# A mixture-of-experts kernel whose routed experts take groups of 512 tokens in place of tiles of 128

## The reference, cut to what matters

```python
# x is (8, 512, 512), cond (8, 512), all float32; 8 blocks of 512 tokens
ae = layernorm(cond) * ln_g + ln_b
xw = gelu(ae @ cw1 + cb1) @ cw2 + cb2            # (8, 2*512*8): x_a, x_b of rank 8
layer = base + einsum('bdr,bkr->bdk', x_a, x_b)
x = x + (x + einsum('btc,bco->bto', x, layer))   # x1, (4096, 512) as tokens

shared = silu(x @ w1) * (x @ w3) @ w2            # 512 -> 1024 -> 512
s = sigmoid(concat(x, cond) @ router_W)          # (4096, 8)
top2 of s + router_bias; gates = the two s, divided by their sum
h = gelu(x @ W1e[e]); y = h @ W2e[e]             # 8 experts, 512 -> 512 -> 512
routed = sum over the two chosen experts of gate * y
x = x + (shared + routed) / 3
```

## Time and profile before

| | us |
|---|---|
| median of three runs | 1197.51 |
| lowest to highest | 1196.04 to 1203.25 |
| the profiled execution, its own time | 1202.75 |
| its span, first to last instruction | 1200.9 |
| TensorE busy | 1160.2 (97%) |
| VectorE, ScalarE, GpSimd busy | 416.4, 287.8, 188.1 |

### The profile page before, as it was taken

How to read it: one execution, slowest core, us unless ns; L and a number is a source line. 1 busy time by engine, 2 the same in 40 slices (tenths; PEclk the granted TensorE clock), 3 DMA queues, 4 the chain that set the end, 5 groups by cost and what they waited for, 6 DMA issues and landing times.

```text
span 1200.9 us, 18241 instructions
## 1 busy us (share of the span) xinstructions
PE 1160.2 (97%) x5762; PEld 935.4 (78%) x5763; DVE 416.4 (35%) x812; ACT 287.8 (24%) x498; POOL 188.1 (16%) x207
## 2 busy tenths in 40 slices
PE   6999898899999999999999998999999999999998
PEld 5666676778788888888888887888888888888887
DVE  4104653535233333333333334233333314233334
ACT  2212453521222222222222222121211112121211
POOL 2002165642510000000000003202020010202020
PEclk8999999899999999999999999999999999999999
DMA  8562589895332222222222224404031130404031
GB/s 309 227 239 95 207 299 347 289 306 162 129 118 83 79 87 79 79 87 79 82 84 83 83 79 123 175 1 175 1 100 74 39 136 0 175 0 175 0 125 49
DMA packets 70480, 151.82 MB, mean 126 GB/s; under 512 B 9753, under 2 KB 18457, under 8 KB 68658
## 3 DMA queue, kind: packets, MB, share of 16 engines
q1 hardware_dynamic: 57666, 111.55, 26.9%
q0 software_dynamic: 12784, 39.86, 9.4%
HBM read 88.73 MB, written 62.65 MB: 126 GB/s over the span
## 4 chain that ended last, share of the span: by engine, by line
PE 91%; DVE 4%; DMA 2%; POOL 1%; issue 1%; ACT 1%; SPq 0%; DVEq 0%; ACTq 0%
PE L L1375 7%; PE L L1377 7%; PE L L1376 7%; PE Rb L1377 7%; PE Rb L1375 7%; PE Rb L1376 7%; PE M L1375 5%; PE M L1376 5%; PE M L1377 5%; PE K L1376 5%; PE K L1375 5%; PE K L1377 5%; PE Rb L1465 3%; PE K L1703 2%; PE K L1660 2%; PE M L1403 2%
## 5 line engine op out<-in xcount | busy, mean ns | idle before, releaser
L752 POOL DMA_INDIRECT yb<-ys_d,pos_fix x64 | 61.2, 957 | 326.6 <-DVE xres L1324 308.6
L1375 PE MATMUL L<-weh,xgh 128*128 x260 | 107.6, 414 | 1.8 <-issue 1.8
L1276 DVE TENSOR_TENSOR xgl<-K,xgh 128x512 fp32r<-128x512 f32 x66 | 45.7, 692 | 173.4 <-ACT xgh L897 173.4
L1375 PE MATMUL Rb<-weh,hTh 128*128 x256 | 105.5, 412 | 0.0
L1375 PE MATMUL K<-x1h,w13h 128*128 128x512 f32 x256 | 101.6, 397 | 3.0 <-DVE x1l L1355 3.0
L1375 PE MATMUL M<-w2h,gTh 128*128 128x512 f32 x256 | 102.3, 399 | 2.3 <-DVE gTl L460 2.3
L1377 PE MATMUL L<-weh,xgl 128*128 x260 | 102.7, 395 | 0.0
L1376 PE MATMUL L<-wel,xgh 128*128 x260 | 102.5, 394 | 0.0
L1376 PE MATMUL K<-x1l,w13h 128*128 128x512 f32 x256 | 102.0, 398 | 0.0
L1376 PE MATMUL M<-w2l,gTh 128*128 128x512 f32 x256 | 101.9, 398 | 0.0
L1377 PE MATMUL M<-w2h,gTl 128*128 128x512 f32 x256 | 101.8, 398 | 0.0
(11 more groups left out here) (238 smaller groups left out, 2146.1 us busy)
## 6 DMA issues: line engine op xcount, KB each, us to landing
xr<-xs_d SPq DMA_DIRECT2D x68, 256.0 KB, 2.6
w2c<-in_L_cond_w_dram SPq DMA_DIRECT2D x8, 2048.0 KB, 8.5
ys_d<-yo SPq DMA_DIRECT2D x64, 256.0 KB, 2.1
xtok<-in_x_dram SPq DMA_DIRECT2D x32, 256.0 KB, 7.4
x_d<-x1tok SPq DMA_DIRECT2D x8, 1024.0 KB, 7.9
xres<-x_d SPq DMA_DIRECT2D x8, 1024.0 KB, 9.5
x1T_d<-xp SPq DMA_DIRECT2D x7, 1024.0 KB, 4.6
out_dram<-xres SPq DMA_DIRECT2D x7, 1024.0 KB, 4.8
```

The lines of the kernel that those rows point to most:

```text
L752: pool.indirect_dma_start(out=yb[:, c, :], out_offset=None, in_=ys_d, in_offset=bass.IndirectOffsetOnAxis(ap=pos_fix[:, c:c + 1].bitcast(U ...
L1276: tt(xgl[:].rearrange("p k n -> p (k n)"), TX[:], xgh[:].rearrange("p k n -> p (k n)").bitcast(F32), ALU.subtract).then_inc(xg_lo, 1)
L1375: mm(o, ah, bh_, start=start, stop=False)
```

## The change

Experts take groups of GR = 512 tokens. In place of the rows, GpSimd scatters token numbers (4 bytes) into `idx_d`; for each group it loads 512 numbers and gathers the rows from `x1_d` (4 indirect DMAs) into `xg`. SP spreads `xg` over `xr` by 16 DMAs of 32 partitions each, such that VectorE's transposes of 32 x 32 blocks finish the turning (the columns of x1 lie permuted in `x1_d` for this). The first product has W1 as the stationary operand and gives h already turned, so TensorE does no transposes. Each group loads W1 and W2 of its expert anew, in four quarters each, which ScalarE and VectorE split. The sum goes to `total`, apart from `xres`, and its first term is added in four parts of 128 columns. `pass_group(g, n)` does group g and prepares n = g + 1.

```diff
-    TILES = (N * TOPK + E * (P - 1)) // P
+    GR = TT * P
+    REGION = N + GR
+    GROUPS_MAX = (N * TOPK + E * (GR - 1)) // GR
...
+        def groups(eng, body):
+            last = value(eng, LAST, 0, GROUPS_MAX - 1, 1)
+            with eng.Fori(0, last) as g:
+                body(g, g + 1)
+            body(last, None)
...
@@ SP
-            def load_rows(t, slot):
-                row = value(sp, ROW, t, E * REGION)
-                sp.dma_start(xr[:, slot], xs_d[ds(row, P), :]).then_inc(xr_in[slot], 16)
+            def load_e1(g, m):
+                row = value(sp, EROW, g, (E - 1) * KC)
+                sp.dma_start(weraw[:, m].rearrange("p (k n) -> p k n", k=KC),
+                             w1e_view[:, ds(row, KC), m * P:(m + 1) * P]).then_inc(weraw_in[m], 16)
+            def spread_rows(g):
+                sp.wait_ge(xg_in, g * (16 * TT) + 16 * TT)
+                for j in range(4):
+                    for i in range(4):
+                        sp.dma_start(xr[32 * j:32 * j + 32, :, i], xg[32 * i:32 * i + 32, :, j * P:(j + 1) * P]
+                                     ).then_inc(xr_in, 16)
+            def load_group(g, n):
+                    sp.wait_ge(xt_f, n * TT)
+                    spread_rows(n)
+                    for m in range(KC):
+                        sp.wait_ge(e2_lo, g * KC + m + 1)
+                        load_e1(n, m)
+                    for m in range(KC):
+                        sp.wait_ge(e1_lo, n * KC + m + 1)
+                        load_e2(n, m)
...
+                store_y(g, 0)
+                store_y(g, 1)
@@ GpSimd
-                            out=xs_d, out_offset=bass.IndirectOffsetOnAxis(ap=pos_int[:, c:c + 1].bitcast(U32), axis=0),
-                            in_=x1tok[i][:, t, :], in_offset=None).then_inc(scat[i], 16)
+                            out=idx_d, out_offset=bass.IndirectOffsetOnAxis(ap=pos_int[:, c:c + 1].bitcast(U32), axis=0),
+                            in_=tokid[:, n:n + 1], in_offset=None).then_inc(ids_out, 16)
+            for t in range(N * TOPK // P, GROUPS_MAX * TT):
+                pool.dma_start(ys_d[t * P:(t + 1) * P, :].rearrange("r (k c) -> r k c", k=KC), zero_src).then_inc(ys_zero, 16)
...
+            pool.wait_ge(S.sum_ps, TT)
+            def gather_rows(g):
+                row = value(pool, ROW, g, E * REGION - GR)
+                pool.dma_start(idx[:], idx_d[ds(row, GR), :].rearrange("(t p) o -> p (t o)", p=P),
+                               allow_slow_non_contiguous=True).then_inc(idx_in, 16)
+                pool.wait_ge(idx_in, g * 16 + 16)
+                for t in range(TT):
+                    pool.indirect_dma_start(
+                        out=xg[:, t, :], out_offset=None, in_=x1_d,
+                        in_offset=bass.IndirectOffsetOnAxis(ap=idx[:, t:t + 1].bitcast(U32), axis=0)).then_inc(xg_in, 16)
+            def gather_group(g, n):
+                    pool.wait_ge(xr_in, n * 256)
+                    gather_rows(n)
@@ ScalarE
+            def pass_group(g, n):
+                cut_e2(g, 0)
+                cut_e2(g, 1)
+                gelu(g, 0)
+                cut_e2(g, 2)
+                gelu(g, 1)
+                cut_e2(g, 3)
+                    cut_e1(n, 0)
+                gelu(g, 2)
+                    cut_e1(n, 1)
+                gelu(g, 3)
+                    cut_x(n, 0)
...
@@ VectorE
+            def turn_rows(g, t):
+                dve.wait_ge(xr_in, g * 256 + 256)
...
+                nc.vector.transpose(xt[:, t % 2].rearrange("p c (i n) -> p i c n", i=4),
+                                    xr[:, t].rearrange("p i (c f) -> p i c f", c=KC)).then_inc(xt_f, 1)
@@ TensorE
+            def mm1(g):
+                pe.wait_ge(xg_lo, g * TT + TT)
+                for m in range(KC):
+                    pe.wait_ge(e1_lo, g * KC + m + 1)
+                    pe.wait_ge(y_sb, g * TT + (m - TT + 1 + Y_FREE))
+                    for k in range(KC):
+                        last_mm = mm3(G[m][:], e1h[:, k, cols], e1l[:, k, cols], x1h[:, k], x1l[:, k], k == 0, k == KC - 1)
+            def mm2(g):
+                for s in range(2):
+                    for m in range(KC):
+                        if s == 0:
+                            pe.wait_ge(ht_lo, g * KC + (m + 1 + H_FREE))
+                            pe.wait_ge(e2_lo, g * KC + m + 1)
+                        for t in (2 * s, 2 * s + 1):
+                            last_mm = mm3(G[t][:], hTh[:, m, rows], hTl[:, m, rows], e2h[:, m], e2l[:, m], m == 0, m == KC - 1)
```

More of the change, by code:

```diff
@@ L293, in build @@
         x1_out = [sem(f"x1_out{i}") for i in range(6)]
-        scat = [sem(f"scat{i}") for i in range(6)]
+        idx_zero = sem("idx_zero")
+        ids_out = sem("ids_out")
         tabs = sem("tabs")
@@ L738, in _ @@
+            gather_rows(0)
+            def gather_group(g, n):
+                if n is not None:
+                    pool.wait_ge(xr_in, n * 256)
+                    pool.wait_ge(xg_in, n * (16 * TT))
+                    gather_rows(n)
+            last = groups(pool, gather_group)
             pool.wait_ge(tabs, 3)
+            pool.wait_ge(ys_zero, 16 * (GROUPS_MAX * TT - N * TOPK // P))
             for s in range(2):
-                pool.wait_ge(y_out[s], pairs * 16)
-            pool.wait_ge(y_ps, pairs * 2 + 1)
+                pool.wait_ge(y_out[s], last * 16 + (16 + YO_FREE))
@@ L933, in fblock, with cut_x1 @@
+            def cut_x1(b):
                 for c in range(KC):
                     nc.scalar.copy(x1h[:, c], x1raw[:, c * T:(c + 1) * T]).then_inc(xf_hi, 1)
+            after = {h: lambda h=h: cut_piece(UP_PIECES + 1 + h) for h in range(PIECES - UP_PIECES - 1)}
+            after[HC - 2] = lambda: [cut_e1(0, m) for m in range(KC)]
+            ffn_act(act, S, 0, True, after)
+            act.sem_inc(y_sb, Y_FREE)
+            for t in range(TT):
+                cut_x(0, t)
+            act.wait_ge(S.g_lo, HC)
@@ L935, in fblock @@
+            groups(act, pass_group)
+            def fblock(b):
+                if not first(b):
+                    act.wait_ge(x1raw_in, b * 16 + 16)
+                    act.wait_ge(F.v_ps, b * HC)
+                    cut_x1(b)
                 ffn_act(act, F, b, first(b))
@@ L950, in tables @@
             tt, ts, red = nc.vector.tensor_tensor, nc.vector.tensor_scalar, nc.vector.tensor_reduce
[L951 to L954 removed]
+            cnt, nt, ends, past, rows, t9 = (tw[:, i] for i in (0, 1, 2, 3, 4, 9))
+            col = [tab[:, i:i + 1] for i in range(COLS)]
@@ L1306, in prepare, with fused @@
                 dve.wait_ge(xres_in, m * 16 + 16)
+                if not first(m):
+                    dve.wait_ge(out_st, m * 16)
+            def fused(t, part, scale, n, done_):
+                if n is not None:
+                    dve.wait_ge(acc, n)
+                    ins = nc.vector.scalar_tensor_tensor(out=total[:, t], in0=part, scalar=scale, in1=total[:, t],
+                                                         op0=ALU.mult, op1=ALU.add)
+                else:
+                    for j in range(4):
+                        ins = nc.vector.scalar_tensor_tensor(
+                            out=total[:, t].rearrange("p (c j f) -> p j c f", j=4, c=KC)[:, j],
+                            in0=part.rearrange("p (c j f) -> p j c f", j=4, c=KC)[:, j], scalar=scale,
+                            in1=xres[:, t].rearrange("p (j c f) -> p j c f", j=4, c=KC)[:, j],
+                            op0=ALU.mult, op1=ALU.add)
+                ins.then_inc(done_, 1)
             def add_shared(t, of, n, done_):
@@ L1726, in fblock, with pass_group, banks_f @@
+            pe.sem_inc(y_ps, Y_FREE)
+            pe.wait_ge(tab_in, 16)
+            pe.wait_ge(S.silu, HC)
+            pe.wait_ge(S.g_f, HC)
+            def pass_group(g, n):
+                mm1(g)
+                mm2(g)
+            last = groups(pe, pass_group)
+            def banks_f(h, i):
+                t = G.index((U, V)[i][h])
+                pe.wait_ge(y_sb, last * TT + (t + 1 + Y_FREE))
             def fblock(b):
-                ffn(F, b, (lambda h, i: None) if first(b) else None, lambda k: pe.wait_ge(xf_lo, b * KC + k + 1),
+                ffn(F, b, banks_f if first(b) else None, lambda k: pe.wait_ge(xf_lo, b * KC + k + 1),
```

477 lines of the change are left out of this document (211 added, 266 removed).

## The result

The changed kernel took 1308.63 us (median of four runs, 1304.55 to 1313.11), the kernel before 1198.21 in the same series: a ratio of 1.092, 95% interval 1.087 to 1.097. Slower, where 1184 was forecast, and outside the range of 1160 to 1226.

The account below looks back on a forecast made before the run. TensorE's own work was taken as the bound (91% of the chain). Front -13.1 and routed stage -1.3 made -14.4 us: 1183.1 against the median of 1197.51, given as 1184, range 1160 to 1226.

Parts of the forecast that it names:

- P: Routed stage: time from a group's first matmul to the next group's, forecast 24.2 us, bounds 22.4 and 27.1.
- 16 copies at 0.42: SP's queue in each group: the spreading copies are issued 0.42 us apart, from 1.95 to 8.65.
- The upper bound of 0.60: SP's spreading copies: a pitch of 0.60 us, from four loads behind others, giving a period of 27.1.
- my two idles of 0.7: TensorE in each group: two idles of about 0.7 us, before the matmuls on h 2 and h 3.
- rival C: SP's queue behind the store of y: pitch 0.60, period 27.1, time 1230 (1210 to 1250), slower than before; chance 0.19.
- a round of gather and spreading: Beside SP's chain in each group: next gather and spreading take 20.6 us a round, under the period of 24.2.
- The 7.07 us go: Front, near 205.5: TensorE's 7.07 us idle vanishes as the weight piece lands earlier; part of the front's -13.1.
- numbers of 4 bytes are free: Front: 64 row scatters become scatters of 4-byte numbers; front -13.1 us, bounds 0 and -13.1.
- The hole before group 0: TensorE idle between shared pass and group 0: 27 us, bounds 24 and 31, plus 2.0 for the clock.
- The sum over the shared blocks: Shared blocks: first adds in four parts cost VectorE 2.2 us more per block, covered by matmuls; 475 us kept.
- the 28 zero stores at nothing: GpSimd's queue in the shared pass: 28 zero stores of y, 26 us beside 66 of matmuls, cost nothing.
- Group 0: Routed stage's first group: its spreading begins at 6.0 us instead of 1.95, so it takes 28.3.

Follow-up runs that it names:

- copy128: Changed kernel with its 16 spreading copies a group going from 128 partitions to the same 128 instead of 32 to 32: 1304.9 us, ratio 1.077.
- split: Changed kernel with 8 of the 16 spreading copies of a group issued from GpSimd's queue instead of SP's: 1218.9 us, ratio 1.003.
- warm: Changed kernel with 24 more matmuls in each group, where TensorE would idle waiting for h 2: 1295.5 us, ratio 1.066.
- order: Changed kernel with ScalarE's W1 casts moved behind the gelus and VectorE's cuts of h ahead of the turns: 1272.5 us, ratio 1.047.
- hybrid: Changed kernel's groups and first product, but rows scattered as before and loaded by SP straight from DRAM, without numbers, gathers or 16 copies: 1171.0 us, ratio 0.965.
- ids_apart: Changed kernel with each scattered 4-byte number in 512 bytes of its own, number buffer not zeroed: 1294.9 us, ratio 1.066.
- ids_64: Changed kernel with scatters writing 64 bytes of zeros for each number, side by side, buffer not zeroed: 1300.2 us, ratio 1.069.
- ids_512: Changed kernel with scatters writing 512 bytes of zeros for each number, buffer not zeroed: 1301.4 us, ratio 1.072.
- ids_half: Changed kernel with 32 of its 64 scatters of numbers, those of the second choice left out: 1274.3 us, ratio 1.049.
- ids_wait: Changed kernel with GpSimd waiting after every fourth scatter of numbers until all have landed: ratio 1.134.
- ids_none: Changed kernel without the 64 scatters of token numbers, every gather fetching row 0: 1275.2 us, ratio 1.051.
- hybrid_order: Kernel that scatters rows and loads groups straight from DRAM, with W1 casts behind gelu 3 and cuts of h ahead of turns: 1149.0 us, ratio 0.947.

## Why the prediction was wrong

*The way to P was right, its longest term was not.* In us after the start of the group at 514.95, forecast and measured: last copy of y done 0.8 and 0.8; copies begun 1.95 and 2.1; **copies issued 8.65 and 12.4**; first quarter of W1 issued 9.35 and 13.6; cast 12.15 and 16.3; h 2 cut 14.7 and 18.8. The step that failed is "16 copies at 0.42": they took 0.645 each. The price was taken from loads out of DRAM; no copy from one place of on-chip memory to another stands in the trace of before. The upper bound of 0.60 was the better number, and the reason for the lower, that SP's queue is nearly empty, had nothing to do with it: SP took 0.586 or more for each of the 256 copies, and 0.60 in the other form too (copy128). This is 3.6 of the 4.1 us by which the cut of h 2 is late against the forecast; the split run shows that this chain is the one that counts.

*What no term covered* is the clock. I charged 2.0 for it once, behind the hole, and nothing in the period, where my two idles of 0.7 were short. The idle of 5.0 to 5.4 is followed by half clock in every group. P = 21.8 of matmuls + 5.2 idle + 2.4 at half clock = 29.4 (at least 1.7 of the 2.4 shown by the warm run). Against the forecast of 24.2 the idle is 3.4 more, the clock 2.4 more, and the matmuls 0.6 less. So rival C, which named the pitch of 0.60, said 27.1 and 1230 and was too low as well. One idle appeared instead of two: while TensorE waited for h 2, h 3 came in.

*What the forecast had beside the chain* was too short as well: a round of gather and spreading, 20.6 forecast, takes 27 (order). It did not bind in the changed kernel. With the copies at 0.42 it would be an estimated 27.0 - 3.6 = 23.4, only just under the 24.2.

*The front.* "The 7.07 us go" rested on the row scatters' bytes. Something of the gain is there in the kernel with no scatters at all: its pass starts 11 us before that of the kernel before on the first chip, where 13.1 were forecast (and probably more against the kernel before on its own chip). The step that failed is that numbers of 4 bytes are free: 64 of them cost 34 us. The forecast bounded this step by 0 from above, so no case of the range held a front slower than before. By the count of writes, 64 x 128 as in the row scatters, there was no ground to take them at nothing.

*The hole before group 0* came out inside its bounds, 30.9 between 24 and 31, and the 5.0 of hybrid shows that the late gather made it. Of the 3.9 over the 27, 15 x 0.225 = 3.4 are the same copies. *The turn* of 512 columns took 0.70 as forecast. *The sum over the shared blocks* (475 forecast, 473 measured) and *the 28 zero stores at nothing* held: in ids_apart they stand inside a shared pass of 67.1 us without an idle. *Group 0* (34.9 for 28.3) has the same two errors, once more: one idle of 8.8 and 4.0 at half clock.

What stays open: by which way scatters delay the front. Neighbouring writes slow the transfers, but without that the front is nearly as late; the bytes of a write and the plain count don't explain it. What the kernels with normal transfers do show is increments that come late. In ids_apart ScalarE's cast of four transposes, the last of which ended at 165.0, began at 174.24; SP's next load, which waits for the same increment, began in the same instant, and GpSimd's wait ended 0.7 later:

```profile
164.34 0.70 PE L1472 MATMUL K<-ident,xtok 128*128 128x128 f32 x4 [2.53 <-issue]
...
174.24 0.33 SPq L525 DMA_DIRECT2D xtok<-in_x_dram  x1
174.24 0.58 ACT L800 CAST xTh<-K 128x512 fp32r<-128x512 f32 x1 [8.60 <-remote]
...
174.97 0.57 POOL L705 DMA_DIRECT2D SB<-xwh_d  x1 [3.19 <-remote]
```

An increment made by TensorE seems to have reached the others 9 us late, 2.4 after the 16th scatter of a burst was issued. It is not alone: ScalarE's cast and SP's load begin together, 1.3 to 9.2 us after the transposes that both wait for, six times in ids_apart and five times each in ids_64 and ids_512, always between 160 and 205 us. In order and split, which have the changed kernel's own front, it happens twice each, by up to 11.7 us, and the idle of order in the shared pass looks the same; in the changed kernel's own trace, where the loads are late, these increments are not. With bursts of 8 (ids_half), with four outstanding (ids_wait) and without scatters (ids_none) it never happens. That late increments in bursts of 16 are the rest of the 34 us is argued from this, not shown: no run took the bursts apart and left all else in place, and a run with all 64 scatters behind the front gave no time.

## What to carry to other kernels

Price a DMA by what it connects and by its count, and take a price only from a row with the same two ends; sixteen small copies are a chain on the queue that issues them, and two queues halve it. Where a chain of loads feeds the next step, let no work that the present one needs stand behind it on an in-order engine: one reordering of casts gave 2.4 us a group here, and 1.4 in the kernel fed straight from DRAM. Replacing a scatter of rows by a scatter of their numbers saves bytes and not scatters. Groups of 512 were worth 5% once they were loaded in the final layout straight from DRAM and the casts stood in the better order.

## What the runs showed of the hardware

- SP takes 0.60 us to issue a copy of 64 KB between two on-chip buffers, of 32 or of 128 partitions, and 0.34 to 0.42 for the loads of W1 and W2 (256 KB) and the stores of y (512 KB) in the same loop, which have DRAM at one end. Loads of 256 KB into 32 partitions take 0.35 at the median, as this row of hybrid_order shows:

```profile
L600 SPq DMA_DIRECT2D xr<-xs_d x64: 316/348/1470, 304.1 to 635.0; - x64
```

- Four outstanding scatters of 128 neighbouring numbers of 4 bytes keep GpSimd waiting 8.9 us, four of 128 rows of 2 KB 3.4 us. With 64 scatters of 4, 64 or 512 bytes a row the shared pass starts 28 to 41 us later than with none; with rows of 2 KB, in the two hybrid kernels, 23 to 24.
- Scatters of 4-byte numbers that lie side by side keep the DMA engines busy for 0.81 of the time at 165 GB/s; with each number in 512 bytes of its own it is 0.46 at 162 GB/s.
- TensorE with a clock at 1.00 does more in less time: with 24 more matmuls in each group a group takes 27.7 us instead of 29.4.
